# Alignment directives in TensorE's instruction list, last stage of a five-part kernel

## The chip, the cores and the metric

The kernel runs on one core of one Trainium2 chip, as one launch. The metric is the device time of that launch in microseconds (us). The time before is 4657.62 us, the median of three runs (4648.66 to 4662.08).

## What is computed

The input is a tensor of 16 sequences with 256 tokens of 128 channels in float32. Four residual layers work on it. In each one an attention-like branch and a feed-forward branch read a normalised input. Nearly seven tenths of the time go to the last branch, `_L3_ffn_ref`, which is a small transformer of six layers. Cut to its core:

```python
for i in range(DEPTH):                                   # DEPTH = 6
    x = attn_layer(shift_tokens(x), Wqkv[i], q_scale[i], k_scale[i], Wo[i]) + x
    x = ffn_layer(shift_tokens(x), ln_g[i], ln_b[i], W1[i], b1[i], W2[i], b2[i]) + x
...
def attn_layer(x, Wqkv, qs, ksc, Wo):                    # 16 heads of 64
    q, k, v = jnp.split(x @ Wqkv, 3, -1)                 # each to (b, h, n, 64)
    q, k = l2norm(q) * qs, l2norm(k) * ksc
    ...                                                  # rotary tables on q and k
    out = local_attention(q, k, v)                       # windows of 32, each looks at itself and the one before
    return out @ Wo
def ffn_layer(x, g, bln, W1, b1, W2, b2):
    ...                                                  # layer norm over the 128 channels
    a, gate = jnp.split(xn @ W1 + b1, 2, -1)
    return a * jax.nn.gelu(gate, approximate=False) @ W2 + b2
```

## The kernel before

The program is unrolled by hand: every engine has one list of instructions without loops, and semaphores order the engines among each other. The class `Kernel` builds five parts one after the other (`L0`, `L1`, `L2`, `L3a`, `L3f`). The change touches the last one, `L3f`, which computes the six layers above.

One turn `u` of `L3f` is one sequence in one layer, so there are N = 96 turns. The function `pe(i)` writes TensorE's list for two turns at a time, in a fixed order of some 60 calls that was written out by hand, with work of the turns 2i+1 to 2i+5 mixed. I call the piece of TensorE's list from one call of `project_out` for an even turn to the next one a pair. The calls that matter here are these:

- `project(u, x)` (L2626): one of twelve projections of a turn, a 128x512 float32 matmul. On the chip a float32 matmul runs as two passes, each with a weight load of its own, so this is four instructions (two loads, two matmuls).
- `turn_qk` (L2639) and `turn_p` (L2668): transposes of 128x128, four and eight at a time, with one pass each.
- `scores(u, t)` (L2655): 64 matmuls of 32x64, each in two passes, so 256 instructions. It is called twice in a turn, four times in a pair.
- `values(u, t)` (L2682): 32 matmuls of 64x64 in two passes, 128 instructions, also four calls in a pair.
- `project_out(u)` (L2694): eight matmuls with 256 columns in two passes, 32 instructions. It waits for `oT_in`, which ScalarE raises when it has copied the heads' outputs (L2895).
- `ffn_gate`, `ffn_up`, `ffn_out` (L2720, L2727, L2736): nine matmuls with 512 columns in a pair; `centre` and `variance` (L2701, L2707): one small matmul each.

A wait on one semaphore rides on the instruction behind it. Where a call waits on several, the others become separate semaphore instructions in the same list (for example L2615 and L2633 in `project` and `turn_qk`). Counted in the built program, a pair has 970 weight loads, 970 matmuls and 29 or 30 separate waits in the middle of a layer, 1969 or 1970 instructions (up to 1974 at a layer's turn). Where I number places in a pair, place 0 is the first instruction behind `project_out` of the even turn, which is the place of the new directive. By this count the four calls of `scores` take places 124 to 379, 587 to 843, 1073 to 1329 and 1532 to 1787.

Other engines serve these calls: DVE (L3036) and GpSimd (L3219 to L3236) scale and rotate queries and keys, ScalarE squares, copies and exponentiates. The DMA queue of SyncE moves the values into windows and loads weights. TensorE's own instructions also come by DMA: the page lists a queue of kind "instruction" for them.

Of the kernel before, what the change touches and what calls it, by code (L numbers as in the profile page):

```python
# [50 lines left out]
class Kernel:  # L51
# [2359 lines left out]
    def L3f(self):  # L2411
# [11 lines left out]
        N = DEPTH * NSEQ  # L2423
# [23 lines left out]
        halves = ((slice(0, HD), 0), (slice(HD, P), 1))  # L2447
        NSMALL, NSCALES = 3 + 6, 6
        FB = (6, 7, 3)

        got_c, got_m, zeroed, made, got_v, got_wo, got_w1, got_w2, got_small, got_scales, rot_in = self.signals(
            "got_c:16", "got_m:16", "zeroed", "made:4", "got_v:16", f"got_wo:{16 * PAIRS}", "got_w1:16", "got_w2:48", f"got_small:{16 * NSMALL}", f"got_scales:{16 * NSCALES}", "rot_in")
# [147 lines left out]
        def pe(i):  # L2600
            p = nc.tensor

            def project(u, x):
                if not 0 <= u < N:
                    return
                j, t, l = RING.index(x), int(x[1]), u // NSEQ
                before = RING[j - 3]
                if j >= 3 or u:
                    v = u if j >= 3 else u - 1
                    if before[0] == "v":  # L2610
                        p.wait_ge(*v_out.at(v, VV.index(before)))
                    else:
                        p.wait_ge(*normed.at(v, QK.index(before)))
                if j == 0 and l:
                    p.wait_ge(*z_out.at((u - NSEQ) // 2))  # L2615
                if x[0] == "v":
                    half = "ab".index(x[2])
                    w = wqkv[:, 2 * INNER:].rearrange("p (a h e) -> p h a e", h=2, e=HD)[:, half, :, :]
                    if u % NSEQ == 0 and t == 0:
                        p.wait_ge(*got_v.all(l))  # L2620
                else:
                    c = "qk".index(x[0]) * 2 + "ab".index(x[2])
                    w = wqkv[:, c * UNIT:(c + 1) * UNIT]
                    if u % NSEQ == 0 and t == 0:
                        p.wait_ge(*got_qk[c].all(l))
                p.matmul(PS[:, j % 3, :], Z[:, u % NSEQ, t * P:t * P + P], w, start=True, stop=True).then_inc(proj.sem)  # L2626
# [59 lines left out]
            def project_out(u):  # L2686
                if not 0 <= u < N:
                    return
                p.wait_ge(*oT_in.at(u, 1))
                if u % NSEQ == 0:  # L2690
                    p.wait_ge(*got_wo.all(u // NSEQ))
                for c in range(PAIRS // 2):
                    for h in range(2):
                        mm = p.matmul(PS[:, 4, 0:SEQ], wo[:, c, h, :], oT[:, :, c, :, h, :], start=(c + h == 0), stop=(c + h == PAIRS // 2))  # L2694
                mm.then_inc(w_mm.sem)

            def centre(u):
                if not 0 <= u < N:
                    return
                p.wait_ge(*z_attn.at(u))  # L2700
                p.matmul(PS[:, 4, SEQ:2 * SEQ], cmat[:, :], Z[:, u % NSEQ, 0:SEQ], start=True, stop=True).then_inc(c_mm.sem)  # L2701
# [7 lines left out]
            def ffn_gate(u, c):  # L2709
                if not 0 <= u < N or u % 2 == 0:  # L2710
                    return
                i, (o, m) = u // 2, CHK[c]
                if c == 0:
                    p.wait_ge(*fn_in.at(u))
                    p.wait_ge(*s_sub.at(min(u + 2, N - 1), 1))
                    if u % NSEQ == 1:
                        p.wait_ge(*got_w1.all(u // NSEQ))
                if c == 2:
                    p.wait_ge(*qk_in.at(min(u + 2, N - 1), 7))
                p.matmul(PS[0:m, FB[c], :], w1[:, DI + o:DI + o + m], fn[:, :], start=True, stop=True).then_inc(g_mm.sem)  # L2720

            def ffn_up(u, c):
# [3 lines left out]
                p.wait_ge(*g_in.at(i, c))  # L2726
                p.matmul(PS[0:m, FB[c], :], w1[:, o:o + m], fn[:, :], start=True, stop=True).then_inc(a_mm.sem)  # L2727

# [48 lines left out]
            turn_qk(2 * i + 3, 0, 3)  # L2777
            project(2 * i + 4, "k0a")
            centre(2 * i + 1)
            turn_qk(2 * i + 3, 1, 0)  # L2780
            project(2 * i + 4, "k0b")
# [17 lines left out]
            ffn_gate(2 * i + 1, 0)  # L2799
            ffn_gate(2 * i + 1, 1)  # L2800
            project_out(2 * i + 2)
            project(2 * i + 4, "v1b")
            ffn_gate(2 * i + 1, 2)
            project(2 * i + 5, "q0a")
            ffn_up(2 * i + 1, 0)
            ffn_up(2 * i + 1, 1)
            ffn_up(2 * i + 1, 2)
            centre(2 * i + 2)
            project(2 * i + 5, "q0b")
            turn_qk(2 * i + 4, 0, 0)  # L2810
# [12 lines left out]
        def act(i):  # L2823
# [102 lines left out]
            def gelu(u, c):  # L2926
# [6 lines left out]
                if i:  # L2933
                    a.wait_ge(*f_mm.at(i - 1))
                a.activation(gg[0:m, c, :], PS[0:m, FB[c], :], ACT.Gelu, bias=b1[0:m, u // NSEQ % 2, 1, c:c + 1]).then_inc(g_in.sem)
                if c == 2:
# [72 lines left out]
        def dve(i):  # L3009
# [87 lines left out]
            def gated(u, c):  # L3097
# [3 lines left out]
                v.wait_ge(*a_mm.at(i, c))  # L3101
                v.scalar_tensor_tensor(gg[0:m, c, :], PS[0:m, FB[c], :], b1[0:m, u // NSEQ % 2, 0, c:c + 1], gg[0:m, c, :], ALU.add, ALU.mult).then_inc(h_in.sem)

# [164 lines left out]
        for i in range(-4, N // 2 + 3):  # L3268
            pe(i)
            act(i)  # L3270
            dve(i)
            pool(i)
# [76 lines left out]
```

## Time and profile before

| | before |
|---|---|
| median of three runs | 4657.62 us |
| lowest, highest | 4648.66 us, 4662.08 us |
| span of the profiled execution | 4655.4 us |
| TensorE busy | 4360.4 us, 94% |
| GpSimd, DVE, ScalarE busy | 78%, 80%, 70% |

The span is the time from the first to the last instruction of one profiled execution; it lies 2.2 us under the median. Busy time counts an engine's own instructions, not waits, semaphore instructions or the issue of DMAs. "Idle before" is the time in which the engine ran nothing, and the name behind the arrow is what ended it; "issue" means that nothing which the profile shows ended it. Last stage here means the stretch from 1535 us on.

### The profile page before, as it was taken

To read this page: it belongs to the slowest core of one execution; us is meant where nothing else is said; L and a number is where in the kernel's file an instruction comes from. 1 tells how busy PE (TensorE), PEld (TensorE's weight loads), DVE (VectorE), ACT (ScalarE), POOL (GpSimd) and SP (SyncE) were. 2 spreads that over 40 slices of the span, in tenths; PEclk is the share of its full clock that TensorE was granted. 3 is DMA by queue.
4 is the path that set the end of the run, shared out by engine and by line. 5 is a ranking of instruction groups with operands and counts; after the bars stand their busy time and mean duration, and the time that the engine had idled before them with its cause. 6 is when DMAs were issued, how large, how long until landed. Compare 5 with 4: busy or idle time off the path is not lost.

```text
span 4655.4 us, 137933 instructions
## 1 busy us (share of the span) xinstructions
PE 4360.4 (94%) x56640; PEld 2936.9 (63%) x56640; DVE 3703.2 (80%) x5128; ACT 3238.4 (70%) x6002; POOL 3648.6 (78%) x1951
## 2 busy tenths in 40 slices
PE   7889899978887999999999999999999999999998
PEld 4556688854443666666666666666666666666665
DVE  6874476759997888888888788888888788878885
ACT  4666655657774777777777777777777777777775
POOL 2223344469997999988999899989999898989993
PEclk9999999989998999999999999999999999999999
DMA  2000000023331222322233322323223222322222
GB/s 81 2 2 2 2 1 1 1 110 146 146 146 57 67 63 61 80 65 66 58 70 74 71 63 61 79 66 69 58 67 76 69 64 60 78 68 66 59 68 53
DMA packets 164376, 290.47 MB, mean 62 GB/s; under 512 B 44063, under 2 KB 61350, under 8 KB 159654
## 3 DMA queue, kind: packets, MB, share of 16 engines
q1 hardware_dynamic: 162310, 281.40, 23.2%
q8 instruction: 452, 7.41, 0.7%
q14 instruction: 174, 1.43, 0.1%
q10 hardware_dynamic: 1440, 0.24, 0.0%
HBM read 90.16 MB, written 2.62 MB: 20 GB/s over the span
## 4 chain that ended last, share of the span: by engine, by line
PE 57%; issue 4%; DVE 4%; DMA 2%; ACT 1%; SPq 1%; POOL 0%; DVEq 0%; ACTq 0%
PE ps L2626 19%; PE ps L2682 7%; PE ps L2639 7%; PE ps L2694 7%; PE ps L2655 5%; PE ps L2668 3%; PE ps L2720 3%; PE ps L2736 3%; PE ps L2727 3%; DMA L3f_vw<-L3f_v 2%; DVE L3f_ss L3019 1%; PE ps L2701 1%; PE ps L2707 1%; DVE L3f_raw L3036 1%; SPq L2472 1%
## 5 line engine op out<-in xcount | busy, mean ns | idle before, releaser
L3219 POOL TENSOR_TENSOR L3f_t<-L3f_raw,L3f_rot 128x1024 f32<-128x1024 f32 x384 | 1085.3, 2826 | 246.4 <-DVE L3f_raw L3036 242.8
L2626 PE MATMUL ps<-L3f_wqkv,all_z 128*128 128x512 f32 x2304 | 1154.1, 607 | 11.2 <-DVE L3f_raw L3036 8.8
L3236 POOL TENSOR_TENSOR L3f_raw<-L3f_raw,L3f_t 128x1024 f32<-128x1024 f32 x384 | 911.9, 2375 | 7.5
L3228 POOL TENSOR_TENSOR L3f_raw<-L3f_raw,L3f_rot 128x1024 f32<-128x1024 f32 x384 | 909.0, 2367 | 7.5
L2835 ACT ACTIVATE L3f_sqr<-ps 128x512 f32<-128x512 f32 x768 | 453.1, 595 | 295.8 <-PE ps L2626 292.4
L3036 DVE TENSOR_TENSOR L3f_raw<-ps,L3f_ri 128x512 f32<-128x512 f32 x768 | 498.7, 686 | 163.5 <-ACT L3f_ri L2845 154.4
L3019 DVE TENSOR_REDUCE L3f_ss<-L3f_sqr 128x8 f32<-128x512 f32 x768 | 515.6, 679 | 115.6 <-ACT L3f_sqr L2835 112.3
L2639 PEld LDWEIGHTS ps<-all_ident,L3f_raw 128*128 128x128 f32 x3072 | 363.3, 141 | 307.8 <-issue 270.3
L2626 PEld LDWEIGHTS ps<-L3f_wqkv,all_z 128*128 128x128 f32 x2304 | 395.8, 192 | 234.8 <-issue 180.2
L2639 PE MATMUL ps<-all_ident,L3f_raw 128*128 128x128 f32 x3072 | 474.5, 277 | 9.4 <-POOL L3f_raw L3236 3.7
L2682 PEld LDWEIGHTS ps<-L3f_pT,L3f_vw 128*64 128x64 f32 x12288 | 375.3, 138 | 97.0 <-issue 78.6
L2682 PE MATMUL ps<-L3f_pT,L3f_vw 128*64 128x64 f32 x12288 | 401.8, 224 | 6.5 <-ACT L3f_pT L2886 6.5
L2886 ACT ACTIVATE L3f_pT<-ps 64x1024 f32<-64x1024 f32 x384 | 388.9, 1013 | 13.6 <-PE ps L2668 7.6
L2694 PE MATMUL ps<-L3f_oT,L3f_wo 128*128 128x256 f32 x1536 | 356.2, 386 | 20.4 <-DMA L3f_wo<-in_L_ffn_Wo 17.6
L3080 DVE TENSOR_TENSOR L3f_sm<-L3f_sm,L3f_sl 128x1024 f32<-128x1024 f32 x192 | 349.8, 1822 | 0.1
L2694 PEld LDWEIGHTS ps<-L3f_oT,L3f_wo 128*128 128x128 f32 x1536 | 293.4, 194 | 82.1 <-issue 32.1
L2869 ACT ACTIVATE L3f_kT<-ps 128x512 f32<-128x512 f32 x384 | 228.2, 594 | 165.1 <-PE ps L2639 159.9
L2655 PE MATMUL ps<-L3f_kT,L3f_qT 64*32 64x64 f32 x24576 | 301.0, 226 | 33.0 <-issue 32.8
L2655 PEld LDWEIGHTS ps<-L3f_kT,L3f_qT 64*32 64x32 f32 x24576 | 264.6, 105 | 98.3 <-issue 80.9
L2895 ACT ACTIVATE L3f_oT<-ps 128x1024 f32<-128x1024 f32 x192 | 196.9, 1025 | 185.4 <-PE ps L2682 185.4
L2346 POOL TENSOR_TENSOR L3a_db_x<-L3a_dx,L3a_Bs 128x1024 f32<-128x1024 f32 x128 | 300.2, 2369 | 1.6 <-DMA L3a_Bs<-L3a_rows 1.4
L3046 DVE TENSOR_TENSOR ps<-ps,L3f_lmaskb 128x1024 f32<-128x1024 f32 x192 | 235.5, 1226 | 69.2 <-PE ps L2655 67.9
(332 smaller groups left out, 8632.4 us busy)
## 6 DMA issues: line engine op xcount, KB each, us to landing
L3f_vw<-L3f_v SPq DMA_DIRECT2D x1344, 128.0 KB, 2.4
L3a_Bs<-L3a_rows SPq DMA_DIRECT2D x16, 2048.0 KB, 7.1
L3a_Cs<-L3a_rows SPq DMA_DIRECT2D x16, 2048.0 KB, 11.7
L3f_vw<-L3f_v SPq DMA_DIRECT2D x192, 64.0 KB
L3f_wqkv<-in_L_ffn_Wqkv SPq DMA_DIRECT2D x24, 256.0 KB, 4.3
L3f_wqkv<-in_L_ffn_Wqkv SPq DMA_DIRECT2D x6, 512.0 KB, 4.2
L3f_wo<-in_L_ffn_Wo SPq DMA_DIRECT2D x48, 64.0 KB, 2.4
out<-all_x SPq DMA_DIRECT2D x8, 256.0 KB, 3.2
```

The lines of the kernel that those rows point to most:

```text
L2626: p.matmul(PS[:, j % 3, :], Z[:, u % NSEQ, t * P:t * P + P], w, start=True, stop=True).then_inc(proj.sem)
L2639: mm = p.transpose(PS[:, 3, c * P:c * P + P], raw[:, t, (4 * g + c) * P:(4 * g + c + 1) * P], ident[:, :])
L2655: mm = p.matmul(PS[w * WIN:(w + 1) * WIN, 6 + h, a * KEYS:(a + 1) * KEYS], qT[r, t, a, w * WIN:(w + 1) * WIN], kT[r, a, t * P + w * WIN:t ...
L2682: mm = p.matmul(PS[to, 4 + c // 2, (c % 2) * 2 * P + w * HD:(c % 2) * 2 * P + (w + 1) * HD], vw[:, u % 2, t * NW + w, a * HD:(a + 1) * HD] ...
L2694: mm = p.matmul(PS[:, 4, 0:SEQ], wo[:, c, h, :], oT[:, :, c, :, h, :], start=(c + h == 0), stop=(c + h == PAIRS // 2))
L2835: a.activation(sqr[:, i % 2, :], PS[:, j % 3, :], ACT.Square).then_inc(sqr_in.sem)
L2886: op = a.activation(pT[r, t, :, :, h, :].rearrange("p a w q -> p (a w) q"), PS[r, 4:6, :].rearrange("p b (n q) -> p (b n) q", q=WIN), ACT. ...
L3019: v.tensor_reduce(ss[:, 0, i * UH:(i + 1) * UH], heads(sqr[:, i % 2, :]), AX.X, ALU.add).then_inc(ss_in.sem)
L3036: v.tensor_tensor(heads(raw[:, t, g * UNIT:(g + 1) * UNIT]), heads(PS[:, RING.index(x) % 3, :]), ri[:, i * UH:(i + 1) * UH].unsqueeze(2).b ...
L3219: g.tensor_tensor(t.rearrange("p h (b e) -> p h b e", b=2), r.rearrange("p h (b e) -> p h b e", b=2)[:, :, ::-1, :], w[:, 1, :].rearrange( ...
L3228: g.tensor_tensor(r, r, w[:, 0, :].unsqueeze(1).broadcast_to((P, H, HD)), ALU.mult).then_inc(cosined.sem)
L3236: g.tensor_tensor(r, r, t, ALU.add).then_inc(rotated.sem)
```

## The change

A new helper `aligned(u)` writes one directive into TensorE's list. It is called once in `pe(i)`, right behind `project_out(2 * i + 2)`, and so 48 times in all, for the even turns.

```diff
+        FETCHED, BEGIN = 256, 87
...
+            def aligned(u):
+                if not 0 <= u < N:
+                    return
+                p.addr_align(FETCHED, offset=BEGIN)
+
...
             project_out(2 * i + 2)
+            aligned(2 * i + 2)
             project(2 * i + 4, "v1b")
```

The directive itself is not executed. When the program is loaded, it is replaced by so many NOPs (instructions that do nothing) that the next instruction stands 87 places behind a multiple of 256 in TensorE's list. No instruction of the program changes its order.

TensorE's list in the second layer's part of the stage, before, around `project_out` of an even turn (the first column is a running number, L2626 is `project`, L2682 `values`, L2720 `ffn_gate`, L2694 `project_out`, L2727 `ffn_up`):

```order
3624 L2682 MATMUL ps<-L3f_pT,L3f_vw 64x64 x31
3625 L2720 MATMUL ps<-L3f_fn,L3f_w 128x512 [waits L1_r_in,L1_v_mm]
3626 L2720 MATMUL ps<-L3f_fn,L3f_w 128x512
3627 L2694 MATMUL ps<-L3f_oT,L3f_wo 128x256 [waits L1_o_mm]
3628 L2694 MATMUL ps<-L3f_oT,L3f_wo 128x256 x7
3629 L2626 MATMUL ps<-L3f_wqkv,all_z 128x512 [waits L0_rstd]
3630 L2720 MATMUL ps<-L3f_fn,L3f_w 85x512 [waits L1_r2_in]
3631 L2626 MATMUL ps<-L3f_wqkv,all_z 128x512 [waits L1_rstd,L0_rstd]
```

The same place of TensorE's list with the change (line numbers are higher by one to six; the row "ISA" is the directive; semaphores have the names of earlier parts, whose numbers they reuse):

```order
3635 L2726 MATMUL ps<-L3f_fn,L3f_w 128x512 [waits L1_r_in,L1_v_mm]
3636 L2726 MATMUL ps<-L3f_fn,L3f_w 128x512
3637 L2695 MATMUL ps<-L3f_oT,L3f_wo 128x256 [waits L1_o_mm]
3638 L2695 MATMUL ps<-L3f_oT,L3f_wo 128x256 x7
3639 L2701 ISA
3640 L2627 MATMUL ps<-L3f_wqkv,all_z 128x512 [waits L0_rstd]
3641 L2726 MATMUL ps<-L3f_fn,L3f_w 85x512 [waits L1_r2_in]
3642 L2627 MATMUL ps<-L3f_wqkv,all_z 128x512 [waits L1_rstd,L0_rstd]
```

Nothing moved: one row is new, between the last matmul of `project_out` and the first of the next `project`. The lists of the other engines have the same rows as before.

## Rows read from the trace of the kernel before

**Rows 1.** Page, part 1: busy time, share of the span, instructions

```profile
...
PE 4360.4 (94%) x56640; PEld 2936.9 (63%) x56640; DVE 3703.2 (80%) x5128; ACT 3238.4 (70%) x6002; POOL 3648.6 (78%) x1951
...
```

**Rows 2.** Waits of TensorE, 1535 to 4656 us: total us, times, longest us

```profile
...
PE ps L2655 <- issue: 32.8, 24, 2.3
PE ps L2694 <- DMA L3f_wo<-in_L_ffn_Wo: 17.6, 5, 4.2
...
PE ps L2626 <- issue: 1.1, 1, 1.1
...
PE ps L2639 <- issue: 0.5, 1, 0.5
```

**Rows 3.** Timeline of TensorE: start us, us, operation, count, idle time before

```profile
...
3444.41 1.47 PE L2655 MATMUL ps<-L3f_kT,L3f_qT 64*32 64x64 f32 x114
3447.62 0.34 PE L2655 MATMUL ps<-L3f_kT,L3f_qT 64*32 64x64 f32 x14 [1.74 <-issue]
...
```

**Rows 4.** The same, second and fourth call of scores, other pairs

```profile
...
3002.84 0.31 PE L2655 MATMUL ps<-L3f_kT,L3f_qT 64*32 64x64 f32 x6 [1.41 <-issue]
...
2962.65 0.31 PE L2655 MATMUL ps<-L3f_kT,L3f_qT 64*32 64x64 f32 x6 [1.41 <-issue]
...
```

**Rows 5.** The same, first call of scores one pair later

```profile
...
3509.61 1.56 PE L2655 MATMUL ps<-L3f_kT,L3f_qT 64*32 64x64 f32 x128
...
```

**Rows 6.** Page, part 3: queue, packets, MB, share

```profile
...
q8 instruction: 452, 7.41, 0.7%
...
```

**Rows 7.** DMA queues in 3444.9 to 3445.0 us: packets, MB, share

```profile
...
q8 instruction: 1, 0.02, 88.3%
...
```

**Rows 8.** Busy us and instructions of each engine between two such stops

```profile
...
3251.43:3447.62 196.19, 191.94 (x2901) 128.97 (x2902) 165.32 (x233) 144.60 (x255) 179.64 (x73) 0.99 0.28 63
...
```

**Rows 9.** TensorE in five pairs: length, busy, matmuls, clock, DMA share, GB/s

```profile
...
3428.90:3494.10 65.20, 63.46 (x971) 1.00 0.27 63
3494.10:3557.88 63.78, 63.43 (x971) 1.00 0.36 89
4284.03:4349.47 65.44, 63.71 (x972) 1.00 0.27 62
4349.47:4413.25 63.78, 63.30 (x971) 1.00 0.28 64
4413.25:4478.63 65.38, 63.52 (x972) 1.00 0.27 62
...
```

**Rows 10.** Waits of TensorE in the pair from 4349.47 us

```profile
...
PE ps L2668 <- DVE L3f_rs L3095: 0.5, 1, 0.5
```

**Rows 11.** Timeline of TensorE around the directive's place in one pair

```profile
...
2838.45 1.99 PE L2720 MATMUL ps<-L3f_fn,L3f_w 128*128 128x512 f32 x4
2840.27 3.62 PE L2694 MATMUL ps<-L3f_oT,L3f_wo 128*128 128x256 f32 x16
2843.73 1.02 PE L2626 MATMUL ps<-L3f_wqkv,all_z 128*128 128x512 f32 x2
...
```

**Rows 12.** Timeline of ScalarE and of DVE there

```profile
...
2838.57 1.02 ACT L2895 ACTIVATE L3f_oT<-ps 128x1024 f32<-128x1024 f32 x1 [0.86 <-PE ps L2682]
...
2841.13 1.29 DVE L3036 TENSOR_TENSOR L3f_raw<-ps,L3f_ri 128x512 f32<-128x512 f32 x2 [0.37 <-ACT L3f_ri L2845]
```

**Rows 13.** Separate waits of TensorE: count, ns min/median/max, first and last start

```profile
...
L2615 PEldq EVENT_SEMAPHORE  x1: 51/51/51, 2841.9 to 2841.9; - x1
...
L2633 PEldq EVENT_SEMAPHORE  x1: 51/51/51, 2875.9 to 2875.9; - x1
...
```

**Rows 14.** Timeline of TensorE's weight loads, behind directive's place and second wait

```profile
...
2843.51 0.41 PEld L2626 LDWEIGHTS ps<-L3f_wqkv,all_z 128*128 128x128 f32 x2
...
2875.94 0.55 PEld L2682 LDWEIGHTS ps<-L3f_pT,L3f_vw 128*64 128x64 f32 x16
...
```

**Rows 15.** The same view, two waits that stand back to back

```profile
...
L914 PEldq EVENT_SEMAPHORE  x13: 51/51/51, 390.1 to 512.9; - x13
...
L915 PEldq EVENT_SEMAPHORE  x13: 51/51/51, 390.2 to 513.1; - x13
...
```

## Prediction

> **What bounds the kernel now.** I read the page's busy times first, then TensorE's waits in the last stage, then the timeline at the places where it waited for nothing visible, and last the DMA queue that brings instructions. TensorE is busy for 94% of the span, no other engine for more than 80% [rows 1]. In the last stage its idle time is small, and the largest entry of it is not a wait for any engine: 24 stops in front of `scores` matmuls, ended by "issue", take 32.8 us, and two more in other calls take 1.1 and 0.5 us, together 34.4 us in 26 stops [rows 2]. One of them looks like this: in a call of `scores` 114 matmuls run, then TensorE stands for 1.74 us, then the other 14 run [rows 3]. The same happens late in the second and in the fourth call of a pair, six matmuls before its end [rows 4]. One pair after the first example, the same call runs its 128 matmuls in 1.56 us without a stop [rows 5]. The program there is the same, so something that isn't in the program differs from pair to pair.
>
> It is the place of the instruction in the list. The instruction queue moved 452 packets with 7.41 MB [rows 6], 16.4 KB each. The built program has 115,662 instructions for TensorE (two for each of the 56,640 matmuls of [rows 1], and 2,382 waits and drains), so a packet is a block of 256. Between the stops at 3251.43 and 3447.62 us the trace has 2901 matmuls and 2902 loads [rows 8]; with the 87 separate waits that the program has there, this is 23 x 256 within the two ends. Counted through the whole list, all 26 stops fall on instruction 193 or 194 of 256, the first one of a block. The packet that ended the stop of [rows 3] started by 3444.9 [rows 7], 2.7 us before TensorE went on. So a block is fetched only a short time ahead. A pair of 65 us has 7.7 blocks, 8.5 us each, which is slow enough. But a call of `scores` is 256 instructions in about 1.5 us, and when a block lies almost wholly inside one, its successor is late.
>
> **Where the stops fall, and where the change puts the borders.** I number places as in the section on the kernel. The 26 stops lie at 309 to 383 (eleven), 802 to 851 (eight), 1292 (one, 0.27 us) and 1761 to 1787 (six): borders in the last quarter of a call or just behind it. Borders elsewhere never stopped TensorE. A pair is 1969 or 1970 long, so from one pair to the next the borders move by some 80 places, and each pair hits another set. With the change the instruction at place 0 stands at 87 of a block, so the borders are at 169, 425, 681, 937, 1193, 1449, 1705 and 1961 of every pair. 425 is 42 places behind the first zone, 1705 is 56 before the last, 937 is 86 behind the second. The pair from 4349.47 us already has its borders three places from these (166, 422, 678 and so on), by chance. It lasts 63.78 us and has no stop of this kind, only 0.5 us for DVE [rows 9, 10].
>
> **What that gives back.** A stop might be made good later, if TensorE then waited less for others. Three pairs with one stop each (1.74, 1.73 and 1.43 us) last 65.20, 65.44 and 65.38 us, two without last 63.78 us, with the clock granted in full in all five [rows 9]. The excess is 1.42 + 1.66 + 1.60 = 4.68 us for 4.90 us of stops, so 95% of a stop is lost for good. All 26 stops come behind the first directive. Gain: 0.95 x 34.4 = **33 us**.
>
> **What the NOPs cost.** To reach 2048 places, a pair gets 74 to 81 NOPs. Worked through the program, 48 directives make 3942: 179 at the first, 109 at the second, 124 at the last, and 3530 at the other 45, 78.4 each. They pass through the part of TensorE that reads the list and handles waits, its sequencer. They are free as long as it gets through them before the array has worked off what stands ahead. In the pair of [rows 11] ScalarE's copy, for which `project_out` waits, ends at 2839.59 [rows 12]. At that time a matmul of `ffn_gate` and the 32 instructions of `project_out` are ahead of the directive, and the load of place 0 runs at 2843.51 [rows 14]. Can the sequencer put 32 to 34 instructions into the queue at once? The separate wait at 2875.9 is executed [rows 13] while 16 loads, their matmuls and four instructions of a projection, all ahead of it in the list, are still to start [rows 14], so it runs at least 36 ahead. I therefore take that it reaches the directive at about 2839.7, and has 3.8 us of cover. The lower bound is 1.7 us: place 0 waits for DVE's first operation of [rows 12], which ended at 2841.8, and the separate wait at place 8 is executed right after, at 2841.9 [rows 13]. This also says that the sequencer stood idle there until 2841.8.
>
> The trace shows no NOP. The nearest rows bound its price c from both sides. The lower end is 6 ns: 256 loads and matmuls of `scores` pass in 1.56 us [rows 5]. The upper end is 106 ns, near the 0.1 to 0.2 us between two separate waits that stand back to back [rows 15]; their own recorded duration is 51 ns [rows 13, 15]. With 3.8 us of cover each, the NOPs cost 45 x (78.4c - 3.8) + (179c - 3.8) + (109c - 3.8) + (124c - 3.8) us, where a negative bracket counts as zero. At 6 ns this is nothing. At 35 ns only the first two and the last directive exceed the cover, by 3 us. At 48 ns it is 8 us, at 51 ns 19, at 57 ns 44, at 60 ns 54, at 80 ns 133, at 106 ns 235. A separate wait is the nearest row, since a NOP is also the sequencer's alone, but a wait has to look up a semaphore, and a NOP doesn't. [...] I therefore take a value under its 51 ns, 35 ns, in the knowledge that this is the weakest number here.
>
> [...]
>
> **The sum.** Span 4655.4 - 33 + 3 = 4625.4 us; with the 2.2 us between the span and the median this is 4628 us, 0.6% faster. What is late next: the 0.5 us per pair for DVE, and five waits of up to 4.2 us for the next layer's `Wo` [rows 2], which the change leaves.
>
> **Rivals.**
> 1. *NOPs as dear as separate waits.* At 80 ns a NOP the sequencer needs 6.3 us for 78 of them, 2.5 us more than it has, in each pair; the queue runs dry at place 0, and TensorE, which has no slack, loses it: -33 + 133 = +100, 4757 us. At 106 ns it is +202, 4860 us. For it speaks that consecutive waits stand 106 ns apart though they record 51, so much of the price may be the sequencer's turn from one instruction to the next, which a NOP would share. It decides from c = 57 ns on. Against it speaks only that a NOP does nothing. Were the cover 1.7 us, it would decide from 30 ns on.
> 2. *NOPs just over the cover*, 51 to 57 ns: gain and cost meet, 4644 to 4669 us.
> 3. *The directive doesn't align the fetched blocks*, because the loader counts from another origin than the fetch does. Then each pair has the same set of borders, but another one. About half of all offsets would put one or two of them into a zone, with some 1.5 us each in 48 pairs: 72 to 144 us, less the 33, so 4700 to 4770 us; the others would give the forecast.
> 4. *The stops are hidden anyway*, since GpSimd or DVE would hold the pair at its length. The two pairs of 63.78 us speak against it [rows 9]. No change: 4658 us.
>
> **How the numbers follow.** A measurement of this kernel can tell 0.3% (14 us) from no change. Forecast with c under 51 ns: 0.47, all of it faster by over 0.3%. Rival 1: 0.33, slower. Rival 2: 0.13, within 0.3%. Rival 3: 0.03, slower. Rival 4: 0.04, within. So faster 0.47, same 0.17, slower 0.36. The low end is 4620 us, all 34.4 us back with free NOPs, and 3 us of spread. The high end is 4760 us, c at 80 ns, which leaves about 0.15 above it. The likeliest case's own range is 4622 to 4644 us.
>
> **What the profile after would show.** "issue" entries before L2655's successor in the last stage fall from 34.4 us to nearly nothing, and every pair in the middle of a layer lasts 63.8 us, if the first half is right. The instruction queue moves 15 packets more, 467. If the NOPs show, a new idle time stands in front of the projection behind `project_out`, of 78c - 3.8 us in each pair; that it is absent would show the second half right. I am wrong if it is there and over 0.7 us, or if `scores` still stops, then at one and the same place in every pair.

## Result

The changed kernel takes 4732.41 us (median of four runs, 4727.12 to 4740.21), the kernel before 4659.85 us beside it (four runs, 4648.66 to 4665.29). The ratio is 1.0163, with a 95% interval from 1.0145 to 1.0181: slower by 1.6%, where I had forecast 0.6% faster.

The span of the profiled execution is 4725.8 us, 70.4 us longer than before. The page of the changed kernel, parts 1 and 3:

```profile
...
PE 4372.9 (93%) x56640; PEld 2933.2 (62%) x56640; DVE 3715.5 (79%) x5128; ACT 3233.7 (68%) x6002; POOL 3648.0 (77%) x1951
...
q8 instruction: 467, 7.65, 0.7%
...
```

Busy times are as in [rows 1], but for 12.5 us more of TensorE. The instruction queue moved 467 packets in place of the 452 of [rows 6]: 15 packets of 256 are 3840 instructions more. The view of the directive's line shows what they are (count, ns min/median/max, first and last start):

```profile
...
L2701 PEldq NOP  x3941: 13/13/13, 1531.4 to 4671.2; - x198
...
```

The trace has no record of the ISA row itself at this line, only the 3941 NOPs (I had worked out 3942), in 48 rows. It also has all 56,640 loads, all 56,640 matmuls and the 2382 waits and drains, so the places can be counted in it. From the end of each row of NOPs to the end of the next there are 2048 instructions, in all 47 cases; in the middle of the stage these are 970 loads, 970 matmuls, and 29 waits with 79 NOPs, 30 with 78 or 34 with 74. By the same count all 26 stops of the kernel before lie at 193 of 256, the first place of a block. The first instruction behind the NOPs lies at 24 in all 48 pairs, 87 places on (193 + 87 - 256). Where the directive has another offset, the instruction behind it moves as well: to 130 with 193 (e2_bad_borders, at its 44 stops there), to 20 with 83 (e4_after_scores), to 99 with 162 (e5_nops_after_scores). At what point on the way from the built list to the chip the NOPs come in, the trace doesn't show.

TensorE's waits in the last stage, changed kernel (total us, times, longest us):

```profile
...
PE ps L2627 <- issue: 91.1, 47, 9.6
PE ps L2669 <- DVE L3f_rs L3102: 15.5, 36, 0.5
PE ps L2695 <- DMA L3f_wo<-in_L_ffn_Wo: 13.9, 5, 4.0
...
PE ps L2726 <- issue: 4.9, 1, 4.9
...
PE ps L2683 <- issue: 0.2, 1, 0.2
```

Compare [rows 2]. The 32.8 us in front of `scores` (L2655 before, L2656 now) are gone to the last stop, and of the other two nothing is left. In their place stands one entry of 91.1 us in front of `project` (L2627) and one of 4.9 us in front of `ffn_gate` (L2726), 48 stops in all: one for each directive. A stop of 0.2 us in front of `values` (L2683) is new. Taken together, idle time ended by "issue" went from 34.4 to 96.2 us. This is 61.8 of the 70.4 us. TensorE's 12.5 us more of busy time for the same matmuls (mean granted clock 0.982 in place of 0.984) are the rest, less some 4 us of other idle time.

The timeline of TensorE around one directive in the changed kernel, as [rows 11] shows it for before, and the view of the directive's line there (count, ns min/median/max, first and last start):

```profile
...
2870.68 1.99 PE L2726 MATMUL ps<-L3f_fn,L3f_w 128*128 128x512 f32 x4
2872.50 3.62 PE L2695 MATMUL ps<-L3f_oT,L3f_wo 128*128 128x256 f32 x16
2877.97 1.10 PE L2627 MATMUL ps<-L3f_wqkv,all_z 128*128 128x512 f32 x2 [1.85 <-issue]
...
```

```profile
...
L2701 PEldq NOP  x79: 13/13/13, 2872.1 to 2877.9; - x79
...
```

The profile shows the NOPs. 79 of them stand between 2872.1 and 2877.9 us, and the projection's first matmul starts right behind the last one, at 2877.97, after TensorE's array has been idle for 1.85 us. So the sequencer needs (2877.9 - 2872.1) / 78 = 74 ns from one NOP to the next (74.2 to 76.8 ns over the 48 rows of NOPs, 75.7 in the mean, from the unrounded starts; I use 75.5 below), although the trace records 13 ns as the duration of each. The length of the padding varies by itself from pair to pair, which gives the same price a second way. A pair with 74 NOPs and a pair with 81:

```profile
...
3075.23 1.10 PE L2627 MATMUL ps<-L3f_wqkv,all_z 128*128 128x512 f32 x2 [1.49 <-issue]
...
```

```profile
...
1744.40 1.10 PE L2627 MATMUL ps<-L3f_wqkv,all_z 128*128 128x512 f32 x2 [2.00 <-issue]
...
```

From 74 to 79 to 81 NOPs the idle time goes 1.49, 1.85, 2.00 us: 73 ns for each NOP more. What the queue covers is the difference, 81 x 0.0755 - 2.00 = 4.1 us. The timeline above has it directly: the first NOP is at 2872.1, and the array runs dry at 2877.97 - 1.85 = 2876.12, 4.0 us later. This holds for most pairs (4.0 to 4.2 us in 41 of the 48); in four the cover was 5.2 to 5.3 us and the stop only 0.6 to 0.8 us.

A pair in the middle of a layer now lasts 65.8 us, in place of 63.78 without a stop [rows 9] (columns: length, TensorE busy and matmuls, granted clock, DMA share, GB/s):

```profile
...
2877.90:2943.70 65.80, 63.56 (x970) 1.00 0.27 62
...
```

### The profile page after: what moved, and what is told of

Read it like the earlier page. It is cut to its first block, busy times and chain, and to the rows that moved or that the text cites. A ratio compares the mean times of both kernels' runs of the same rounds, so it can differ in the third digit from the quotient of the medians.

```text
span 4725.8 us, 141874 instructions
## 1 busy us (share of the span) xinstructions
PE 4372.9 (93%) x56640; PEld 2933.2 (62%) x56640; DVE 3715.5 (79%) x5128; ACT 3233.7 (68%) x6002; POOL 3648.0 (77%) x1951
## 4 chain that ended last, share of the span: by engine, by line
PE 55%; issue 6%; DVE 4%; DMA 2%; ACT 1%; POOL 1%; SPq 1%; DVEq 0%; ACTq 0%; POOLq 0%
PE ps L2627 18%; PE ps L2683 7%; PE ps L2695 6%; PE ps L2640 6%; PE ps L2656 4%; PE ps L2669 3%; PE ps L2726 3%; PE ps L2742 3%; PE ps L2733 3%; DMA L3f_vw<-L3f_v 2%; DVE L3f_ss L3026 1%; DVE L3f_raw L3043 1%; PE ps L2707 1%; PE ps L2713 1%; SPq L2473 0%
## 5 line engine op out<-in xcount | busy, mean ns | idle before, releaser
L2627 PE MATMUL ps<-L3f_wqkv,all_z 128*128 128x512 f32 x2304 | 1157.3, 608 | 101.0 <-issue 91.1
L2627 PEld LDWEIGHTS ps<-L3f_wqkv,all_z 128*128 128x128 f32 x2304 | 391.7, 192 | 338.9 <-issue 287.4
L2683 PEld LDWEIGHTS ps<-L3f_pT,L3f_vw 128*64 128x64 f32 x12288 | 376.3, 138 | 97.4 <-issue 78.7
L2683 PE MATMUL ps<-L3f_pT,L3f_vw 128*64 128x64 f32 x12288 | 403.1, 224 | 6.6 <-ACT L3f_pT L2893 6.4
L3087 DVE TENSOR_TENSOR L3f_sm<-L3f_sm,L3f_sl 128x1024 f32<-128x1024 f32 x192 | 363.8, 1895 | 0.1
L2656 PEld LDWEIGHTS ps<-L3f_kT,L3f_qT 64*32 64x32 f32 x24576 | 262.9, 105 | 62.5 <-issue 45.1
L2656 PE MATMUL ps<-L3f_kT,L3f_qT 64*32 64x64 f32 x24576 | 294.8, 226 | 0.3
L1981 PE MATMUL ps<-L3a_hc,all_ident 128*128 128x512 f32 x512 | 250.0, 636 | 37.5 <-DVE L3a_hc L2254 23.7
```

The costliest lines, as they stand in the source:

```text
L2656: mm = p.matmul(PS[w * WIN:(w + 1) * WIN, 6 + h, a * KEYS:(a + 1) * KEYS], qT[r, t, a, w * WIN:(w + 1) * WIN], kT[r, a, t * P + w * WIN:t ...
L2683: mm = p.matmul(PS[to, 4 + c // 2, (c % 2) * 2 * P + w * HD:(c % 2) * 2 * P + (w + 1) * HD], vw[:, u % 2, t * NW + w, a * HD:(a + 1) * HD] ...
```

## Experiments

I go on calling the places where the kernel before stopped zones (309 to 383, 802 to 851, 1292 and 1761 to 1787 of a pair), and the explanation so far theory A: the change does both things at once. It takes away all stops at the borders of fetch blocks, which were worth some 33 us, and puts 75 ns of sequencer time for each NOP in their place, of which 4.1 us are covered in each pair. Against it stood that the new borders themselves cost (rival C), that the stops were never a matter of borders (D, E), and for the variants with a branch, that a branch costs a fetch (B, F). These letters are those of the expectations, not the numbers of the prediction's rivals. The kernel before had medians of 4656.34 and 4657.30 us beside the two sets of runs.

**The same borders without the NOPs.** The directive is written with `max_nops=0`. The trace then has no NOP at its line but 48 branches, one for each directive (second view below), and the instruction queue moved 467 packets, as in the changed kernel: the padding is still in the list and is passed over.

```diff
-                p.addr_align(FETCHED, offset=BEGIN)
+                p.addr_align(FETCHED, offset=BEGIN, max_nops=0)
```

> The changed kernel, but the padding is branched over (one branch is executed in place of up to 255 NOPs); the fetch blocks' borders stay where the change puts them. Theory A (the change takes away 33 us of stops, and loses 96 us because 79 NOPs of 75.5 ns each, measured in the trace after, outlast the 4 us that the queue covers): the NOPs are gone, the stops stay away, and if a branch takes less than the 4 us of cover the time is 4660 - 33 = about 4627 us. Rival B (a branch makes the sequencer fetch its target anew): the idle time in front of the projection is what a fetch takes less the cover, anything from 0 to some 4 us in each of 48 pairs, 4627 to 4820 us. Rival C (the loss of the change comes from where the borders lie now, not from the NOPs): as the change, about 4732 us.

4615.83 us, ratio to before 0.9905 (0.9874 to 0.9937). Waits of TensorE in the last stage, and the directive's line:

```profile
...
PE ps L2669 <- DVE L3f_rs L3102: 15.1, 36, 0.5
...
PE ps L2695 <- DMA L3f_wo<-in_L_ffn_Wo: 11.3, 5, 2.6
...
PE ps L2683 <- issue: 1.8, 3, 0.9
...
```

```profile
...
L2701 PEldq COMPARE_BRANCH  x48: 173/292/394, 1534.4 to 4559.2; - x48
...
```

No stop in front of `scores` or of the projection is left (three short ones in front of `values`, 1.8 us, are new; counted in the trace they lie at place 937, one of the borders). A pair in the middle of a layer lasts 63.7 us:

```profile
...
2887.27:2951.01 63.74, 63.31 (x971) 1.00 0.28 64
...
```

The branches are there, 48 of them with 292 ns in the median, and their time is under the cover. Rival C falls: the borders lie where the change puts them, and the kernel is some 117 us faster than the changed one. With the NOPs gone, the rest of the change is a gain of 40 us, a little more than the 33 us that I had given it. In the profiled executions 32.6 us are idle time ended by "issue" (34.4 to 1.8 us). Most of the rest is TensorE's busy time for the same matmuls, 9.6 us shorter at a granted clock of 0.986 in place of 0.984. The clock of the kernel before lay between 0.980 and 0.987 from run to run, so I don't credit the change with this.

**Two short paddings in place of one long.** The directive stands behind `project_out` of either turn, with 32 to 43 NOPs each; borders at 169, 425, 681, 937, then 1153, 1409, 1665, 1921.

```diff
-        FETCHED, BEGIN = 256, 87
+        FETCHED, BEGIN, SECOND = 256, 87, 138
...
-                if not 0 <= u < N:
+                if not 2 <= u < N - 3:
...
-                p.addr_align(FETCHED, offset=BEGIN)
+                p.addr_align(FETCHED, offset=BEGIN if u % 2 == 0 else SECOND)
...
             project_out(2 * i + 1)
+            aligned(2 * i + 1)
```

> Two directives in a pair in place of one, behind the project_out of either turn, so that each makes 32 to 43 NOPs in place of 79 (3562 in all; none for the first turn and the last three); borders at 169, 425, 681, 937, 1153, 1409, 1665, 1921, all outside the zones. Theory A: 43 NOPs of 75.5 ns take 3.2 us, less than the 4 us of cover, so nothing is idle behind project_out; the stops stay away but for one or two in the first pair: 4660 - 33 + 2 = about 4629 us. If the cover behind the odd turn's project_out is shorter (say 2 us), +1.2 x 45 = 4683 us. Rival C (the loss comes from the borders, or from NOPs at any number): 4700 us or more.

4624.23 us, ratio 0.9929 (0.9904 to 0.9955). Waits of TensorE in the last stage and the directive's line:

```profile
...
PE ps L2695 <- DMA L3f_wo<-in_L_ffn_Wo: 17.1, 5, 4.4
...
PE ps L2656 <- issue: 1.2, 1, 1.2
...
PE ps L2683 <- issue: 0.2, 1, 0.2
```

```profile
...
L2701 PEldq NOP  x3561: 13/13/13, 1596.2 to 4504.3; - x198
...
```

3561 NOPs are executed here, nine tenths of the changed kernel's number, and no time is idle behind them: 43 x 75.5 ns = 3.2 us is under 4.1 us. (The cover behind the odd turn's `project_out` isn't measured; it was enough.) So it isn't the number of NOPs that costs, but the part of each row of them that outlasts the queue. The one stop of 1.2 us is in the first pair, which has no directive.

**The NOPs where nothing covers them.** The directive moves behind the last call of `scores` in the pair.

```diff
-        FETCHED, BEGIN = 256, 87
+        FETCHED, BEGIN = 256, 83
...
             scores(2 * i + 3, 1)
+            aligned(2 * i + 2)
...
-            aligned(2 * i + 2)
```

> The changed kernel with the directive moved from behind project_out to behind the last call of scores of the pair (offset 83, so the borders stay at the same places, and the number of NOPs is 79 again; 92 at the first). A call of scores leaves the array only some 0.3 us of work in the queue. Theory A: almost the whole 6.0 us of the NOPs is idle time of TensorE, 5.7 us in place of 1.85 in each pair: 4732 + 3.85 x 48 - 3 = about 4914 us. Rival C (the NOPs' place has no part in it): about 4732 us.

5059.78 us, ratio 1.0863 (1.0828 to 1.0899), 146 us over what I expected. Waits of TensorE in the last stage:

```profile
...
PE ps L2627 <- issue: 272.0, 47, 8.5
PE ps L2656 <- issue: 69.5, 47, 2.4
...
PE ps L2683 <- issue: 8.3, 1, 8.3
...
```

272.0 us in 47 stops is 5.8 us each: the whole of the NOPs but 0.2 us, as expected. The rest has two causes. I had miscounted the borders. The padding moves what stands ahead of it too, so they lay at 248, 504 and so on up to 1784 in each pair, and 1784 is in the last zone: 47 stops of 1.5 us, as theory A says of that place. And the granted clock fell. TensorE from 2500 to 3500 us in this kernel, then in the changed one:

```profile
...
2500.00:3500.00 1000.00, 895.86 (x13122) 0.94 0.26 61
...
```

```profile
...
2500.00:3500.00 1000.00, 959.85 (x14618) 1.00 0.29 67
...
```

The same variant with the borders where they should be (offset 162 in place of 83) keeps the two apart:

> The directive with its 79 NOPs behind the last call of scores of a pair, as in e4_after_scores, but with offset 162, so that the borders really stay at 169 to 1705 (and 1882 in place of 1961). In e4_after_scores they had moved to 248 to 1784, and 1784 lies in a zone: 47 stops there took 69.5 us, the NOPs another 272 us, and TensorE's granted clock was 0.94 in the middle of the stage. Theory A: the scores stops go, 47 x 5.8 us idle behind the NOPs stay, and 13 to 20 us for the longer paddings at both ends. Theory A with clock G (5.8 us of idle time alone make the clock fall): 4616 (e1_branch) + 273 + 16 + about 60 us of lost clock = about 4965 us, clock near 0.95. Theory A with clock H (it takes the stop and the NOPs together, 7.3 us): about 4905 us, clock 0.99.

4978.81 us, ratio 1.0685 (1.0665 to 1.0705). Waits of TensorE in the last stage, and the clock's row:

```profile
...
PE ps L2627 <- issue: 271.1, 47, 13.4
...
PE ps L2683 <- issue: 8.5, 2, 8.0
...
```

```profile
...
2500.00:3500.00 1000.00, 915.59 (x13511) 0.95 0.27 62
...
```

The stops in `scores` are gone with the border at 1784. The NOPs' stops stay, 271.1 us, and the clock is still at 0.95. TensorE around one of these stops, and then length, busy time and clock of the stretch from the clock's fall on and of the rest of the pair:

```profile
...
2608.25 1.68 PE L2656 MATMUL ps<-L3f_kT,L3f_qT 64*32 64x64 f32 x128
2615.11 5.29 PE L2627 MATMUL ps<-L3f_wqkv,all_z 128*128 128x512 f32 x6 [5.18 <-issue]
...
```

```profile
...
2613.30:2620.00 6.70, 4.89 (x6) 0.50 0.00 0
2620.20:2684.90 64.70, 60.78 (x965) 1.00 0.28 64
...
```

The granted clock falls to 0.50 at 2613.27 us, 3.3 us after TensorE has come to a stand, and stays there for 6.8 us, so the projections behind the stop run at it (over the 48 such stops the fall comes 1.7 to 5.2 us after the stop begins): six matmuls of 512 columns take 5.29 us, where six in e4_after_scores (from 2594.81 us on) took 2.84. The variant with a branch at the same place (e7_branch_after_scores, below) has the clock at 1.00 in this stretch. With 1.85 us of standing still in a pair the changed kernel's clock stayed at 1.00 too (its row under e4_after_scores). Against e1_branch the kernel loses 363 us, of which idle time ended by "issue" explains 271.1 + 8.5 - 1.8 = 278 us. The other 85 us go to the clock: TensorE's busy time for the same 56,640 matmuls is 4457.6 us in place of 4350.8, 107 us more, and other waits are some 20 us shorter for it.

**Bad borders.** The changed kernel with `BEGIN` = 193, so with borders at 63, 319, 575, 831 and so on, two of them in zones:

> The changed kernel with 193 in place of 87: almost the same number of NOPs (3792 for 3942, 29 at the first directive for 179), but the borders fall on places 63, 319, 575, 831, 1087 and so on of each pair, two of them (319 and 831) in the zones where the kernel before stopped. Theory A: two stops in every pair, about 1.8 us in the first call of scores and 1.4 us in the second, 3.2 x 48 = 153 us more than the change, less 9 us for the shorter first padding: about 4876 us. Rival D (the stops have nothing to do with the borders of fetch blocks, and the change lost them by chance or by the NOPs' pause): 4732 - 9 = about 4723 us, no stops.

4794.77 us, ratio 1.0299 (1.0261 to 1.0336), 62 us over the changed kernel where I expected 144. Waits of TensorE in the last stage:

```profile
...
PE ps L2656 <- issue: 71.5, 65, 2.2
PE ps L2627 <- issue: 71.2, 43, 3.9
...
PE ps L2726 <- issue: 4.7, 1, 4.7
...
PE ps L2683 <- issue: 0.2, 1, 0.2
```

Stops in `scores` are back, 65 of them with 71.5 us, so rival D falls. But 48 pairs with two borders in zones should give 96, and they are shorter than I took them, 1.1 us each. The idle time behind the NOPs is also 20 us less than in the changed kernel, where I had allowed 9. A border in a zone doesn't stop TensorE each time. The same without NOPs and with one border in the middle of the first zone, 353, is the cleaner case:

```diff
-        FETCHED, BEGIN = 256, 87
+        FETCHED, BEGIN = 256, 159
...
-                p.addr_align(FETCHED, offset=BEGIN)
+                p.addr_align(FETCHED, offset=BEGIN, max_nops=0)
```

> e1_branch (no NOPs are executed) with 159 in place of 87: borders at 97, 353, 609, 865, 1121, 1377, 1633, 1889 of every pair; 353 is in the middle of the first zone, the others are outside. It prices the stops alone. Theory A: one stop of about 1.8 us in each of 48 pairs, 95% of it lost: 4616 + 82 = about 4698 us. Rival E (the stops are absorbed, and e1_branch is faster than the kernel before for another reason): about 4616 us.

4681.53 us (median of eight runs), ratio 1.0048 (1.0030 to 1.0065), 66 us over e1_branch. The profiled execution is the longest of the eight, 17 us over the median. Waits of TensorE in the last stage:

```profile
...
PE ps L2656 <- issue: 56.5, 36, 1.8
...
```

36 of 48 pairs stop there in `scores`, 1.57 us each, and the first pair in front of a projection, 1.8 us; counted in the trace all 37 lie at place 353. Rival E falls: moving the borders alone, with nothing else changed, takes the kernel from 0.95% faster to 0.5% slower than before. Two neighbouring pairs show why not all of them stop. In the first one `scores` runs through; its block's packet was under way at 2877.1, 4.6 us before the border at 2881.7. In the next it stops; the packet came at 2944.8, 2.5 us before TensorE went on. Timeline and instruction queue of the first pair, then of the second:

```profile
...
2880.48 1.56 PE L2656 MATMUL ps<-L3f_kT,L3f_qT 64*32 64x64 f32 x128
...
```

```profile
...
q8 instruction: 1, 0.02, 37.9%
...
```

```profile
...
2944.14 1.45 PE L2656 MATMUL ps<-L3f_kT,L3f_qT 64*32 64x64 f32 x114
2947.28 0.34 PE L2656 MATMUL ps<-L3f_kT,L3f_qT 64*32 64x64 f32 x14 [1.69 <-issue]
...
```

```profile
...
q8 instruction: 1, 0.02, 34.6%
...
```

So in these pairs it goes by how early the fetch starts. Over all 48 pairs, it starts 2.3 to 2.7 us before TensorE goes on where it stopped, which is 0.4 to 1.1 us before the border, and 3.0 us or more before the border where it did not stop. I take it that the sequencer's entry into the block ahead starts the fetch. The NOPs support this where they show the sequencer itself: in the changed kernel three rows of NOPs run over a border, and the next packet of the instruction queue starts 0.7 to 2.0 us after the border's NOP (1538.04 and 1539.17 us at the first directive). Why the sequencer enters the block sooner in some pairs, I have not tested.

**A branch where nothing covers it**, at the place of e5_nops_after_scores and with the same borders:

> The branch of e1_branch behind the last call of scores, where the queue holds only some 0.3 us of work, same borders as e5_nops_after_scores. It prices a branch without cover. Theory A (a branch is one more instruction of the sequencer, 0.3 us as the trace records it): 0.1 to 0.3 us idle in each pair, 4616 + 5 to 15 = 4620 to 4631 us. Rival B (its target is fetched anew, which 4 us of cover hid in e1_branch): 2 to 4 us in each pair, 4710 to 4810 us.

4619.63 us, ratio 0.9918 (0.9890 to 0.9945). The directive's line:

```profile
...
L2701 PEldq COMPARE_BRANCH  x48: 170/170/1248, 1526.7 to 4546.4; - x48
...
```

170 ns in the median, and no stop of 0.15 us or more, from which on they are listed, stands behind it. A branch over the padding of a pair needs no cover, and rival B falls for it. The 1248 ns are those of the first branch, at 1526.7 us, the only one here whose padding is 170 long and runs over a border. In e5_nops_after_scores the NOPs at the same border stand 1.14 us apart. I take both for a wait for the next block; no run tests it.

**Another good offset**, with a branch over a border (`BEGIN` = 56, borders at 200, 456 and so on):

> e1_branch with 56 in place of 87: borders at 200, 456, 712, 968, 1224, 1480, 1736 of every pair, and one border inside the skipped padding at place 0, so that the branch leads into the next block. All are outside the zones (1736 is 25 places before the last one). Theory A (any offset outside the zones is as good): 4616 us, as e1_branch. Rival F (a branch over a border makes the sequencer wait for a fetch): up to some 2 us in each pair behind the projection's place, up to 4710 us.

4624.04 us, ratio 0.9927 (0.9906 to 0.9947), which the intervals don't part from e1_branch. The directive's line:

```profile
...
L2701 PEldq COMPARE_BRANCH  x48: 292/292/332, 1533.6 to 4569.0; - x48
...
```

292 ns, as in e1_branch, where the branches lead over no border; rival F falls. (Why this place of the list has 292 ns in the median with the offsets 87 and 56, and 170 ns with 159 in e6_branch_bad, is open.) Two stops are left in `scores`:

```profile
...
PE ps L2656 <- issue: 2.5, 2, 1.5
...
```

One is in the first pair with a directive and one in the last whole pair. By these two runs (4615.83 and 4624.04 us) the offset matters little outside the zones, but for these; 87 is nothing special.

## Why the prediction was wrong

The reading of the kernel before held. **Where the stops are and why**: borders of 256 instructions in the last quarter of a call of `scores`. e6_branch_bad puts the stops back by moving nothing but the borders. **What they are worth**: I had 33 us. e1_branch gained 40 us by the medians (interval 29 to 59 us), 32.6 us of it in idle time ended by "issue". The pairs there came out as foretold: 63.7 us in the middle of a layer, with up to 0.5 us of waiting for DVE in 36 of them.

**The cover** was the better half of the cost: 3.8 us taken, 4.1 us measured.

**The price of a NOP** is the step that failed. I had set its bounds at 6 and 106 ns, with 57 ns as the point from which the cost decides. (My formula gives 42 us there and not the 44 I wrote, and reaches the 33 us of gain at 55 ns.) Then I chose 35 ns, with the reason that a NOP has no semaphore to look up and so must cost less than the 51 ns recorded for a wait. In two points the trace bears this out: the NOPs are recorded on the sequencer as the separate waits are (`PEldq` in both views), and with less, 13 ns for 51. It doesn't show what a wait spends on its semaphore, and no run shows the 35 ns: that was my estimate. The reason took the recorded duration of an instruction for the time that the sequencer spends on it. [rows 15] already showed the difference: two waits back to back record 51 ns each and stand 106 ns apart. Some 55 ns of that belong to no instruction's duration. A NOP is recorded with 13 ns and stands 75.5 ns from the next, 62 ns over its duration. 55 ns plus any duration at all would have put the price beyond the break-even of 55 ns, and the forecast at "no change or slower". With 75.5 ns and 4.1 us my own sum gives 45 x (5.92 - 4.1) + 9.4 + 4.1 + 5.3 = 101 us for the NOPs and 4659.85 + 101 - 33 = 4728 us; measured are 4732. It is rival 1, at a price a little under the 80 ns that I had worked out for it. That the time lies within my range is owed to this rival, which set the upper end, and not to the mechanism that I forecast.

The other rivals: the directive does align the fetched blocks (3), since no pair of the changed kernel stopped in `scores`, and the first instruction behind the NOPs lies 87 places behind the border in each pair. The stops were not hidden (4): e1_branch is faster, and e6_branch_bad 66 us slower than it. A price of 51 to 57 ns (2) is excluded by the 75.5 ns.

## What to carry to other kernels

In this kernel a short call with many tiny instructions (256 in 1.56 us) outran the fetch of its own code, whose packet started 2.3 to 2.7 us before TensorE went on (e6_branch_bad). The sign was idle time ended by nothing visible, 26 times at the same instruction number modulo 256. Aligning the list cured it (32.8 us of stops in `scores` before, none in e1_branch), and a branch over the padding (170 to 292 ns in the median) was the way to do it, not NOPs; split into rows that the queue covered (3.2 us for 4.1 us), the NOPs left no idle time behind them either. And what a NOP cost its sequencer was to be read from the distance between two in a row (75.5 ns), not from its recorded duration (13 ns).

## What the runs showed of the hardware

- NOPs of TensorE stand some 75.5 ns apart with 13 ns recorded, separate waits 106 ns apart with 51 ns recorded (11 of the 13 of [rows 15]; the other two 197 ns), while weight loads and matmuls pass at 6 ns each [rows 5]. A branch is recorded with 168 ns (e6_branch_bad) to 394 ns (e1_branch), and once with 1.25 us (e7_branch_after_scores).
- TensorE's queue held 4.1 us of work ahead of the sequencer behind `project_out` in most pairs (changed kernel: 4.0 to 4.2 us in 41 of 48).
- In e5_nops_after_scores TensorE stood still for 5.8 us in each pair, and the granted clock fell to 0.50 toward the end of the stop and behind it, 0.95 in the mean; in the changed kernel it stood for 1.85 us and the mean stayed at 1.00 (both 2500 to 3500 us).
- Of 48 borders at place 353, 37 stopped TensorE: 36 in `scores`, with 1.57 us each, and one in front of a projection, with 1.8 us (e6_branch_bad). The fetch started 2.3 to 2.7 us before TensorE went on.
